# A fused attention and feed-forward kernel: scores products of one item in one stretch, and a new order of work on all engines

## What is computed

```python
def _layer(x, wqkv, qs, ksc, wo, lg, lb, w1, b1, w2, b2):
    h = shift_token(x)
    q, k, v = jnp.split(h @ wqkv, 3, axis=-1)          # 8 heads of 64
    q = l2norm(q) * qs
    k = l2norm(k) * ksc
    q, k = rotary_xpos(q, k)
    o = local_attention(q, k, v)                       # windows of 128 rows: own and the one before
    x = x + o @ wo
    h = shift_token(x)
    h = (h - h.mean(-1)) / jnp.sqrt(h.var(-1) + 1e-05) * lg + lb
    a, g = jnp.split(h @ w1 + b1, 2, axis=-1)          # hidden width 682
    return x + (a * gelu(g)) @ w2 + b2

x = x + xattn(layernorm(x), ctx_768)
y = layernorm(x)
for l in range(2): y = _layer(y, ...)
return x + y
```

## Time and profile before

| | us |
|---|---|
| median of 3 runs | 1509.66 |
| lowest and highest | 1508.18, 1509.79 |
| the profiled execution | 1507.65 |
| its span, first to last instruction | 1505.9 |
| TensorE busy in the span | 1425.0 (95%) |
| VectorE, ScalarE, GpSimd busy | 1102.2, 938.2, 745.3 |
| mean granted TensorE clock | 0.976 |

### The profile page before, as it was taken

One profiled execution on the slowest core, in us unless ns is written; L12 is line 12 of the kernel. 1 busy time (PEld: TensorE's weight loads), 2 busy tenths in 40 slices (PEclk: granted clock), 3 DMA queues, 4 the chain that ended last, 5 costly groups with the idle time before them and its releaser, 6 DMA issues.

```text
span 1505.9 us, 33288 instructions
## 1 busy us (share of the span) xinstructions
PE 1425.0 (95%) x11616; PEld 1261.7 (84%) x11616; DVE 1102.2 (73%) x3054; ACT 938.2 (62%) x2670; POOL 745.3 (49%) x571
## 2 busy tenths in 40 slices
PE   4999999867999999999999899999999999999996
PEld 3888888746888988889888788888888888888886
DVE  3766666446788878788877777877878888888854
ACT  3776666524666666666666666756666666666661
POOL 1111121044556666666665556556555665566632
PEclk9999999888999999999999999999999999999998
DMA  6311111200001100000001020111111111111001
GB/s 193 104 62 45 49 54 46 85 29 19 21 28 35 35 28 27 27 27 27 27 27 31 19 72 28 35 36 35 38 36 49 36 34 34 34 41 34 28 28 30
DMA packets 50819, 62.87 MB, mean 42 GB/s; under 512 B 8514, under 2 KB 32424, under 8 KB 50728
## 3 DMA queue, kind: packets, MB, share of 16 engines
q1 hardware_dynamic: 50728, 61.68, 13.0%
HBM read 37.86 MB, written 16.78 MB: 36 GB/s over the span
## 4 chain that ended last, share of the span: by engine, by line
PE 73%; DVE 13%; ACT 5%; issue 4%; DMA 2%; SPq 2%; POOL 1%; DVEq 0%; POOLq 0%; ACTq 0%
PE pb L519 33%; PE pb L803 6%; PE pb L789 6%; PE pb L765 5%; PE pb L734 5%; PE pb L749 5%; PE pb L827 4%; DVE p_t L1364 2%; PE pb L580 2%; PE pb L568 2%; PE pb L618 2%; PE pb L622 2%; DVE r_sin L1351 2%; DVE n_sq L1331 1%; DVE p_t L1378 1%
## 5 line engine op out<-in xcount | busy, mean ns | idle before, releaser
L1550 POOL TENSOR_TENSOR n_inv<-n_cl,half_neg 128x16 f32<-128x16 f32 x64 | 210.9, 3296 | 179.3 <-DVE n_cl L1336 175.7
L1057 ACT ACTIVATE p_t<-p_t,s_nm 128x128 f32<-128x128 f32 (+1 forms) x512 | 227.1, 448 | 27.1 <-DVE s_nm L1364 25.2
L519 PE MATMUL pb<-h_hi,w_hi 128*128 128x256 f32 x704 | 208.6, 296 | 2.4 <-DVE h_lo L1327 2.4
L519 PE MATMUL pb<-h_hi,w_lo 128*128 128x256 f32 x704 | 199.5, 283 | 0.0
L519 PE MATMUL pb<-h_lo,w_hi 128*128 128x256 f32 x704 | 199.4, 283 | 0.0
L1555 POOL TENSOR_TENSOR r_cos<-r_cos,r_sin 128x1024 f32<-128x1024 f32 x64 | 154.4, 2412 | 59.4 <-DVE r_sin L1351 59.4
L1048 ACT ACTIVATE pt_t<-pb 128x512 f32<-128x512 f32 x192 | 114.4, 596 | 101.4 <-PE pb L749 100.2
L1015 ACT ACTIVATE qk_sq<-pb 128x512 f32<-128x512 f32 x128 | 72.3, 591 | 164.4 <-PE pb L519 164.4
L519 PE MATMUL pb<-wqkv_hi,xt_hi 128*128 128x512 f32 x384 | 165.6, 431 | 9.4 <-DVE r_sin L1351 8.5
L1364 DVE CUSTOM_DVE_ANT_0 p_t<-pb,mask_t 128x128 f32<-128x128 f32 (+1 forms) x512 | 151.9, 353 | 26.5 <-PE pb L734 26.2
L1581 POOL TENSOR_TENSOR hg_lo<-hg,hg_hi 128x256 fp32r<-128x256 f32 x192 | 139.4, 747 | 55.7 <-DVE hg_hi L1395 55.7
(11 more groups left out here) (131 smaller groups left out, 3996.3 us busy)
## 6 DMA issues: line engine op xcount, KB each, us to landing
y_state<-x SPq DMA_DIRECT2D x32, 256.0 KB, 2.1
x_cur<-y_state SPq DMA_DIRECT2D x32, 256.0 KB, 2.6
x_res<-y_state SPq DMA_DIRECT2D x32, 256.0 KB, 2.8
x_in<-x SPq DMA_DIRECT2D x16, 256.0 KB, 2.9
x_state<-x SPq DMA_DIRECT2D x16, 256.0 KB, 2.0
x_orig<-x_state SPq DMA_DIRECT2D x16, 256.0 KB, 2.9
out<-x SPq DMA_DIRECT2D x16, 256.0 KB, 2.2
x<-x SPq DMA_DIRECT2D x32, 112.0 KB, 2.3
```

Source lines behind the costliest of these rows:

```text
L519: mm = pe.matmul(dst, s, m, start=(n == 0 and k == 0), stop=(n == len(pairs) - 1 and k == 2))
L1057: e = nc.scalar.activation(pu, pu, ACT.Exp, bias=s_nm[:, j, k:k + 1], scale=-1.0, accum_out=s_sum[:, j, k:k + 1])
L1550: nc.gpsimd.tensor_tensor(n_inv[:, t], n_cl[:, t], half_neg[:], ALU.pow).then_inc(pool_inv, 1)
```

## The change

1. Bank and order of the scores: units 2 and 3 move from banks 3 and 4 to 5 and 6, so `scores(1)` no longer waits for the maxima of units 0 and 1. It waits instead for `dve_x1` of item c, that is for `residual` at the end of the iteration before (bank 6). `scores(2)` waits for the maxima of units 0 and 1, `turn_p(0)` also for that of unit 2 (bank 5), `weigh(0)` also for that of unit 3 (bank 6) and no longer for `dve_x1`.
2. TensorE's order in an iteration is now scores(0), scores(1), project(0,0), scores(2), feed(0), feed(1), project(0,1), turn_p(0), feed(2), project(0,2), feed(3) to feed(5), turn_h, project(1,2), turn_p(1), project(1,1), turn_p(2), project(1,0), turn_p(3), weigh(0), turn_next, turn_p(4), hidden(0), turn_p(5), weigh(1), weigh(2), hidden(1) to hidden(5), out_product(0), the four turn_qk, out_product(1).
3. VectorE: `stats_h` is followed by the sums and `norm_probs` of units 0 and 1; `norm_h` stands ahead of `rotate(a, 0)`; `rotate(a, 1)` stands behind `norm_probs(5)` and behind `squares(a, 1)`; `gate_hi(3)` to `gate_hi(5)` move into the next iteration, between the maxima; `residual` stands ahead of `gate(5)`.
4. ScalarE: exps(0) and exps(1) come first, square(1,0) and square(1,1) behind exps(5) and probs_copy(3), `out_hi` is split in two, gelu(5) stands behind the four `copy_qk`.
5. GpSimd: `inverse_norms(a, 0)` ahead of `add_parts(a, 0)`; `gate_lo(0)` ahead of `kept_rows`; `gate_lo(2)` to `gate_lo(4)` at the end of the iteration, `gate_lo(5)` behind `deviation` of the next.

```diff
-        QKV_PLACE = {(0, 1): 1, (0, 0): 2, (0, 2): 3, (1, 0): 4, (1, 1): 5, (1, 2): 6}
+        QKV_PLACE = {(0, 0): 1, (0, 1): 2, (0, 2): 3, (1, 2): 4, (1, 1): 5, (1, 0): 6}
         W1_BANK = [4, 0, 1, 2, 4, 0]
-        S_BANK = [3, 4, 3, 4, 3, 4]
+        S_BANK = [3, 4, 5, 6, 3, 4]
...
-            def scores(a, b, j):
+            def scores(a, b, c, j):
...
+                elif j == 1:
+                    if c is not None:
+                        pe.wait_ge(dve_x1, at(c, 1, 1))
                 else:
-                    pe.wait_ge(dve_max, at(b, UNITS, 2 * j))
+                    pe.wait_ge(dve_max, at(b, UNITS, 2))
...
             def turn_p(a, b, d, u):
 
                 pe.wait_ge(dve_pn, at(b, UNITS, u + 1))
+                if u == 0:
+                    pe.wait_ge(dve_max, at(b, UNITS, 3))
...
                     pe.wait_ge(act_v, at(b, NT, NT))
-                    if c is not None:
-                        pe.wait_ge(dve_x1, at(c, 1, 1))
+                    pe.wait_ge(dve_max, at(b, UNITS, 4))
...
                 if b is not None:
-                    scores(a, b, 0)
-                if a is not None:
-                    project(a, d, 0, 1)
+                    scores(a, b, c, 0)
+                    scores(a, b, c, 1)
                 if a is not None:
                     project(a, d, 0, 0)
+                if b is not None:
+                    scores(a, b, c, 2)
...
-            def out_hi(b):
+            def out_hi(b, k):
                 act.wait_ge(pe_av, at(b, 3, 3))
-                for k in range(2):
-                    nc.scalar.activation(o_hi[:, 2 * k:2 * k + 2].rearrange("p c t -> p (c t)"), pb[:, 6 + k],
-                                         ACT.Copy).then_inc(act_ohi, 1)
+                nc.scalar.activation(o_hi[:, 2 * k:2 * k + 2].rearrange("p c t -> p (c t)"), pb[:, 6 + k],
+                                     ACT.Copy).then_inc(act_ohi, 1)
...
                 if b is not None:
                     maxes(b, 0)
+                if d is not None:
+                    gate_hi(d, 3)
+                if b is not None:
                     maxes(b, 1)
+                    maxes(b, 2)
+                if d is not None:
+                    gate_hi(d, 4)
                 if c is not None:
                     stats_h(c)
+                if b is not None:
+                    inverse_sums(b, 0)
+                    norm_probs(b, 0)
+                    inverse_sums(b, 1)
+                    norm_probs(b, 1)
+                    maxes(b, 3)
+                if d is not None:
+                    gate_hi(d, 5)
...
-                if a is not None:
+                if a is not None:
+                    inverse_norms(a, 0)
                     add_parts(a, 0)
-                    inverse_norms(a, 0)
```

More of the change, by code:

```diff
@@ L841, in run_l @@
                     feed(c, d, 1)
+                if a is not None:
+                    project(a, d, 0, 1)
                 if b is not None:
-                    scores(a, b, 1)
+                    turn_p(a, b, d, 0)
+                if d is not None:
+                    feed(c, d, 2)
                 if a is not None:
@@ L865, in run_l @@
                     turn_p(a, b, d, 1)
+                if a is not None:
+                    project(a, d, 1, 1)
+                if b is not None:
                     turn_p(a, b, d, 2)
+                if a is not None:
+                    project(a, d, 1, 0)
+                if b is not None:
+                    turn_p(a, b, d, 3)
+                    weigh(b, c, 1 - par, 0)
                 if has_next(a):
@@ L1093, in run_l @@
                 a, b, c, d, par = l_roles(g)
-                if a is not None:
-                    square(a, 0, 0)
-                    square(a, 0, 1)
                 if b is not None:
@@ L1099, in run_l @@
                     exps(b, 1)
+                if a is not None:
+                    square(a, 0, 0)
+                if b is not None:
                     exps(b, 2)
+                    exps(b, 3)
+                if a is not None:
+                    square(a, 0, 1)
+                if b is not None:
+                    probs_copy(b, 0)
                 if a is not None:
@@ L1103, in run_l @@
                 if b is not None:
-                    exps(b, 3)
-                    probs_copy(b, 0)
                     exps(b, 4)
@@ L1109, in run_l @@
                 if a is not None:
+                    copy_v(a, 1, par)
+                if b is not None:
+                    probs_copy(b, 1)
+                    exps(b, 5)
+                if a is not None:
                     square(a, 1, 0)
                 if b is not None:
-                    probs_copy(b, 1)
+                    probs_copy(b, 2)
+                    probs_copy(b, 3)
                 if a is not None:
@@ L1465, in run_l @@
                 if c is not None:
-                    gate(c, 0, layer)
+                    gate(c, 1, layer)
+                    gate_hi(c, 1)
+                    gate(c, 2, layer)
+                    gate_hi(c, 2)
                 if b is not None:
```

122 lines of the change are left out of this document (47 added, 75 removed).

## The result

The changed kernel takes 1525.05 us (median of 4 runs, 1522.98 to 1528.28) against 1508.92 for the kernel before beside it (4 runs, 1507.97 to 1509.79): a ratio of 1.011, 95% interval 1.0096 to 1.0124. It is slower by 16 us where I had forecast 9 us faster, and it lies outside my range of 1493 to 1518. The profiled execution took 1524.42 with a span of 1521.7; before, the span was 1505.9.

The account below looks back on a forecast made before the run. TensorE, busy for the whole steady iteration, was taken to bound the kernel. 29 iterations at -0.37 us give -10.7, with +1.4 for the ends -9.3: from 1509.66 to a median of 1500.4 us, range 1493 to 1518.

Parts of the forecast that it names:

- TensorE's own sequence: TensorE's steady iteration: -0.20 - 0.07 + 0.05 - 0.15 = -0.37 us, a period of 34.92 instead of 35.29.
- The merged block: scores(0) and scores(1) on TensorE in one stretch of 2.05 us, where two blocks of 1.07 stood.
- chain (a): From project(1,0) through the squares to rotate(1), ending at 23.35; hidden(1) asks at 23.7, so 0.35 us to spare.
- chain (b): GpSimd from rotate(1) through add_parts, inverse_norms and norm_qk, ending at 31.1; turn_qk(0) asks at 31.7, 0.6 us to spare.
- rival D: Hand-over chain to rotate(1) 0.35 to 1.1 us longer than counted, without contention; 1518 us at 1.0; chance 0.17.
- the race: From clamp(0), VectorE reaches norm_probs(5) in 3.45 us, GpSimd add_parts(0) in 3.62: VectorE first by 0.17, GpSimd loses 0.5.
- Rival C: norm_probs(5) loses to add_parts(0), rotate(1) ends at 24.9, hidden(1) 1.2 us late; period 36.1, time 1536; chance 0.14.
- The ends: Run's start, end and the boundary between layers, outside the steady iterations: +1.4 us in all, between -2 and +5.
- the boundary: Between the two layers: included in the +1.4 us in all, without a size of its own.
- The end: Last iterations: later gate_hi(5) adds about 2.4 us; fewer gate_lo and earlier scores(2) give back some 1.9.
- the start: At g = 0 GpSimd's chain begins behind squares(0) and clamp(0) instead of rotate(0): about +0.7 us.

Follow-up runs that it names:

- the run of 2: The changed kernel with GpSimd's add_parts(0) also waiting for norm_probs(5), and VectorE's gate_hi(2) moved behind out_lo(1): 1497.22 us, 0.9931 of the kernel before.
- experiment 1: The changed kernel with one more wait, so that GpSimd's add_parts(0) cannot start ahead of norm_probs(5): 1528.88 us, 1.0143 of the kernel before.
- experiment 7: The kernel before with VectorE's norm_probs(5) moved ahead of clamp(1): 1506.09 us in one run.
- experiment 10: The run of 2 with layer 1's weight split moved to iteration 17's end, and gate_hi(5), gate_lo(5) ahead of the statistics in iterations without scores: 1488.56 us.
- experiment 5: The changed kernel with VectorE's norm_probs(5) ahead of split_h_lo instead of behind it: 1610.01 us.

## Why the prediction was wrong

**TensorE's own sequence: right.** I had 34.92; with the collisions gone it is 34.99. The merged block is 2.08 (2.05), hidden(1) comes at t = 23.75 (23.7), rotate(1) ends at 23.39 (23.35), GpSimd at 30.74 (31.1), turn_qk(0) is asked for at 31.74 (31.7), all from the run of 2. So chain (a) had the margin that I gave it (0.36 us), chain (b) had 1.0 instead of 0.6, since its inverse_norms(1) takes 2.91 and not 3.32, and rival D is out.

**The step that failed** is the race in the part on GpSimd and VectorE: "GpSimd needs 0.23 + 3.32 + 0.07 = 3.62", VectorE 3.45, so "VectorE is first by 0.17 us". Measured from the start of clamp(0) (662.62), add_parts(0) begins at +3.11 and norm_probs(5) at +3.59: GpSimd is first by 0.48. VectorE's count was 0.14 short. GpSimd's was 0.51 long: 0.41 of it is the term 3.32 for inverse_norms, which takes 2.91 in its new place, and most of the rest the 0.07 behind it, where add_parts(0) begins 0.05 before the recorded end (665.73 against 665.78). The 0.41 alone turns the order; the 0.14 alone would not have. The row was right and was of another situation. In before both inverse_norms of the iteration began beside a running norm_probs, the second as shown in experiment 7 (636.54 in 636.37 to 637.05), the first here:

```profile
628.62 0.69 DVE L1378 TENSOR_TENSOR p_t<-p_t,s_inv 128x512 f32<-128x512 f32 x1
...
628.73 3.36 POOL L1550 TENSOR_TENSOR n_inv<-n_cl,half_neg 128x16 f32<-128x16 f32 x1 [5.69 <-DVE n_cl L1336]
```

I had the means to see it: for the earlier trace rows I had used the very rule that whoever is second pays, and did not apply it to the row that I summed with. A margin of 0.17 us was no margin when one of its terms was itself the result of a collision that the change removed. Two sums are also off by a little as written, without weight for the outcome: VectorE's terms add up to 3.43 and not 3.45, and turn_qk(0)'s to 31.6 and not 31.7.

**Rival C was right** in place, mechanism and size: norm_probs(5) to the end of add_parts(0), rotate(1) at t = 24.68 (24.9), period 35.99 (36.1). I gave it 0.14. That chance should have been near a half: it stood or fell with 0.17 us out of 3.6. Its price of 1536 was 11 us too high: the loops' iterations cost 0.70 more than before and not 0.87, and the written-out ones at the head of each layer 0.4 (35.68).

**A second collision was not in the prediction at all.** Had VectorE won, rotate(1) would have been on time as in experiment 1, gate_hi(2) would have met norm_qk(1), and by that run the time would have been near 1529 all the same. I had priced the pair where the change puts two steps together, and not those where an earlier rotate(1) does.

**The ends: +1.4 was too small.** In the changed kernel iteration 18 alone costs 4.1 us more than before (42.06 against 37.92). The windows of it and of two stretches inside, TensorE's row at scores(2), and from the kernel before its row at scores(1):

```profile
940.81:982.87 42.06, 37.60 (x288) 33.73 (x287) 31.27 (x82) 27.71 (x63) 20.84 (x14) 0.92 0.09 31
...
947.60:951.40 3.80, 0.12 (x3) 0.06 (x2) 3.80 (x11) 1.25 (x5) 0.72 (x1) 0.87 0.38 140
951.40:955.00 3.60, 3.60 (x23) 3.38 (x24) 3.38 (x14) 2.68 (x11) 2.34 (x4) 0.50 0.02 5
...
951.34 1.01 PE L737 MATMUL pb<-qk_t 64*128 64x128 f32 x6 [3.68 <-DVE s_nm L1370]
...
947.72 0.49 PE L734 MATMUL pb<-qk_t 64*128 64x256 f32 x2 [1.09 <-DVE s_nm L1364]
```

scores(2) now stands near the head and waits for the maxima of units 0 and 1, and these stand behind the split of weights. Before, it was scores(1) that waited for the same maxima, with two projections and two feed pieces ahead of it, and it waited 1.09 us; now only scores(1) and one projection lie ahead, and the wait is 3.68. The idle stretch also goes with a lower clock: TensorE is busy for 0.12 of the 3.80 us up to 951.40, and in the 3.60 us behind it the granted clock is 0.50, that is 1.2 GHz instead of 2.4. The same iteration has 1.00 throughout in before, and in experiment 10, where the wait is gone. The account of the 15.8 us of span: start and iterations 1 and 2 -1.8, iterations 3 to 15 +4.7, 16 to 19 +4.1, 20 to 31 +8.2, the rest +0.6 (a later feed(5) at the very end against a shorter iteration 32). So start, boundary and end are +2.9 together where I had +1.4. The end is what I had (2.4 - 1.9 = 0.5); the start gained 1.8 where I had a loss of 0.7; the boundary is the term that I left in "+1.4 in all" without a row. Experiment 10 takes away the causes at the boundary and at the end in one run, and since the two places lie apart each gain is seen by itself.

Two sections of the Trainium skill bear on these readings. I had cited GPSIMD Engine Reference, section Key points, which names the contention without a price. The Trainium skill's page SBUF — State Buffer, section Who interferes with whom, has the rule that prices it: whichever of the two issues first keeps the shared pair for its whole instruction and the other is fully blocked, and a VectorE instruction with at most one SBUF input outside the two-port modes does not contend. The runs agree (norm_probs(5) takes 0.69 us when it is 0.01 us ahead and 2.90 when it is 0.01 us behind, both in experiment 5), with one exception: inverse_norms, which also has two SBUF inputs, blocked no norm_probs that began while it ran (663.72, 0.69 us, beside 662.87 to 665.78).

## What to carry to other kernels

A duration taken from a trace belongs to its neighbours: before you sum with it, look at what ran beside it on the engine that shares its port, and take the undisturbed value for a place where the neighbour is gone. Where the order of two starts decides over 2 us per iteration, don't price the margin, remove it: one wait on the engine that has time to spare (GpSimd here) makes the order certain, and then look for the next pair that the faster iteration brings together. And walk the exceptional iterations one by one (weight splits, drain): here they were worth 8.7 us, as much as the whole steady gain (29 times 0.31).
